# A spiking transformer layer with a gated expert layer: LIF at full width and new places for side work in the first seven beats

## What is computed

```python
def lif_step(v, x_t):                 # leaky integrate and fire
    v = v + (x_t - v) * TAU_INV       # 0.5
    s = spike(v - V_TH)               # 1.0 where v >= 1
    v = v * (1.0 - s)
    return (v, s)

R, K, V = x @ Wr.T, x @ Wk.T, x @ Wv.T          # per step of time:
    vr, r = lif_step(vr, r_in); vk, k = lif_step(vk, k_in); vv, v = lif_step(vv, v_in)
    h = h * DECAY + k * v                       # 0.9
    y = r * h
x1 = layernorm(residual + y @ Wo.T, ln1_g, ln1_b)
h1 = x1 @ W1.T + b1;  s1 = lif_scan(h1)
h2 = s1 @ W2.T + b2;  ffn_out = lif_scan(h2)
attn = layernorm(x1 + ffn_out, ln2_g, ln2_b)
x = _layernorm(x + attn)
x = _layernorm(x + ffn(x))     # softmax gates, best 2 of 8 experts, renormalised
```

## Time and profile before

| | |
|---|---|
| median of 3 runs | 1058.89 us (1058.12 to 1059.48) |
| the profiled execution | 1059.16 us |
| its span | 1057.40 us, 22664 instructions |
| PE busy | 954.4 us (90%) |
| DVE busy | 952.2 us (90%) |
| ACT busy | 551.1 us (52%) |
| POOL busy | 584.8 us (55%) |

### The profile page before, as it was taken

How to read it: one execution, slowest core, us unless ns; L and a number is a source line. 1 busy time by engine, 2 the same in 40 slices (tenths; PEclk the granted TensorE clock), 3 DMA queues, 4 the chain that set the end, 5 groups by cost and what they waited for, 6 DMA issues and landing times.

```text
span 1057.4 us, 22664 instructions
## 1 busy us (share of the span) xinstructions
PE 954.4 (90%) x7552; PEld 929.2 (88%) x7552; DVE 952.2 (90%) x3847; ACT 551.1 (52%) x1270; POOL 584.8 (55%) x726
## 2 busy tenths in 40 slices
PE   4767789999999999999999999999999999898882
PEld 4667779999999999999999999999999999888882
DVE  6898888999999999999999999999999999989861
ACT  4333333555566555555566655555556655455552
POOL 2011112577666666667666666667766666664452
PEclk8778888999999999999999999999999999999996
DMA  4210112454445454445434544544443454456674
GB/s 162 91 51 31 40 31 51 76 105 96 90 86 111 101 110 102 101 91 108 92 88 95 111 101 103 108 98 94 100 93 86 104 103 98 91 100 128 127 136 90
DMA packets 53974, 99.87 MB, mean 94 GB/s; under 512 B 5985, under 2 KB 5985, under 8 KB 53857
## 3 DMA queue, kind: packets, MB, share of 16 engines
q0 software_dynamic: 32256, 58.73, 32.1%
q1 hardware_dynamic: 16992, 31.30, 9.5%
q10 hardware_dynamic: 4608, 8.39, 2.1%
HBM read 31.29 MB, written 8.39 MB: 38 GB/s over the span
## 4 chain that ended last, share of the span: by engine, by line
PE 63%; DVE 26%; DMA 3%; POOL 3%; issue 3%; ACT 2%; POOLq 0%; DVEq 0%; ACTq 0%
PE ps_e L344 28%; PE ps_proj L344 9%; PE ps_proj L414 9%; PE ps_attn L380 6%; PE ps_proj L420 5%; DVE U L713 5%; DVE V L720 4%; DVE stats L794 4%; DVE h L764 2%; PE ps_proj L399 2%; PE ps_attn L388 2%; DVE x1n L821 2%; DVE x1n L806 2%; DMA acc<-term 1%; PE ps_zx L388 1%
## 5 line engine op out<-in xcount | busy, mean ns | idle before, releaser
L344 PE MATMUL ps_e<-we_hi,x_hi 128*128 128x256 f32 (+1 forms) x1024 | 292.8, 286 | 4.0 <-ACT odd_sum L586 4.0
L344 PE MATMUL ps_e<-we_lo,x_hi 128*128 128x256 f32 (+1 forms) x1024 | 287.1, 280 | 0.0
L344 PE MATMUL ps_e<-we_hi,x_lo 128*128 128x256 f32 (+1 forms) x1024 | 287.1, 280 | 0.0
L720 DVE SCALAR_TENSOR_TENSOR V<-U 128x256 f32<-128x256 f32 (+5 forms) x656 | 249.4, 390 | 0.6
L713 DVE SCALAR_TENSOR_TENSOR U<-V,U 128x256 f32<-128x256 f32 (+5 forms) x656 | 234.9, 368 | 1.8
L549 ACT ACTIVATE U<-ps_proj,cst 128x256 f32<-128x256 f32 x320 | 135.6, 481 | 173.1 <-PE ps_proj L420 89.6
L1111 POOL TENSOR_SCALAR veps<-mv 128x2 f32<-128x2 f32 x128 | 56.5, 441 | 295.3 <-DVE mv L800 295.3
L1125 POOL TENSOR_SCALAR s<-U 128x256 fp32r<-128x256 f32 x208 | 192.4, 950 | 10.5 <-DVE V L720 10.5
L344 PEld LDWEIGHTS ps_e<-we_hi,x_hi 128*128 128x128 f32 x1024 | 192.9, 188 | 4.7 <-ACT odd_sum L586 4.6
L344 PEld LDWEIGHTS ps_e<-we_hi,x_lo 128*128 128x128 f32 x1024 | 193.0, 188 | 0.1
L344 PEld LDWEIGHTS ps_e<-we_lo,x_hi 128*128 128x128 f32 x1024 | 192.4, 188 | 0.0
(11 more groups left out here) (85 smaller groups left out, 2185.9 us busy)
## 6 DMA issues: line engine op xcount, KB each, us to landing
acc<-term POOLq DMA_DIRECT2D x96, 256.0 KB, 3.7
odd_sum<-term POOLq DMA_DIRECT2D x96, 256.0 KB, 3.3
xt<-x_T SPq DMA_DIRECT2D x33, 256.0 KB, 2.9
xa<-x_tok SPq DMA_DIRECT2D x32, 256.0 KB, 4.2
xb<-cst SPq DMA_DIRECT2D x32, 256.0 KB, 2.3
xb<-x_tok POOLq DMA_DIRECT2D x32, 256.0 KB, 6.1
out<-res ACTq DMA_DIRECT2D x32, 256.0 KB, 2.1
term<-w SPq DMA_DIRECT2D x8, 256.0 KB, 5.5
```

The source lines that it names most:

```text
L344: mm = pe.matmul(dst, lhs, rhs, start=(i == 0), stop=(i == n - 1))
L720: v.scalar_tensor_tensor(out=V[:, c0:c1], in0=u, scalar=THRESHOLD, in1=u, op0=ALU.is_lt, op1=ALU.mult).then_inc(done, 1)
```

## The change

- In beats 0 to 4 LIF is issued at full width, one instruction where there were two; the property `halves` and the semaphore `lif_half` go.
- In `FILL` beats the spikes of the first layer no longer stand in slot -1 but one tile each in slots 0 to 7 (beats 3 to 6 have them). In `DRAIN` beats they stay in slot -1.
- In `FILL` the sum of the first norm moves from slot 2 to 6, its statistics from 3, 4 to 7, 8, the aggregation from 5 to 9, the normalisation from 9 to 15, `x1_low` from 15 to 23; the second and third norms' work moves by 1 or 2 slots, most gate steps and `add_e0` by 1.

```diff
-FILL = dict(z_sum=-1, y=(-1,) * 5, spikes_h1=-1, fin_sum=-1,
-            gate=(4, 5, 6, 7, 8, 9, 10, 11, 12, 13, 17, 18), add_e0=(14, 15),
-            ln1_sum=2, ln1_stats=(3, 4), ln1_aggr=5, ln1_norm=9, x1_low=15,
-            ln2_stats=(0, 1), ln2_aggr=2, ln2_scale=(6, 7), ln2_add=8,
-            ln3_stats=9, ln3_aggr=10, ln3_shift=16, x3_low=31,
+FILL = dict(z_sum=-1, y=(-1,) * 5, spikes_h1=0, fin_sum=-1,
+            gate=(5, 6, 7, 8, 9, 10, 11, 12, 13, 14, 17, 18), add_e0=(15, 16),
+            ln1_sum=6, ln1_stats=(7, 8), ln1_aggr=9, ln1_norm=15, x1_low=23,
+            ln2_stats=(1, 2), ln2_aggr=3, ln2_scale=(8, 9), ln2_add=10,
+            ln3_stats=11, ln3_aggr=12, ln3_shift=18, x3_low=31,
             fin_add=24, fin_stats=25, fin_aggr=26, fin_shift=31)
...
-            def lif_part(b, c0, c1, first_half):
+            def lif_part(b, c0, c1):
...
-                done = lif_half if first_half else lif
-                before = 2 * STEPS * b.k if first_half else b.value(2 * STEPS, 0)
+                done = lif
+                before = b.value(2 * STEPS, 0)
...
-                    if b.halves:
-                        dve.wait_ge(lif_half, last)
...
-                if b.has(LAG_S) and b.dve_spikes and slot == at["spikes_h1"]:
-                    spikes_h1(b)
+                if b.has(LAG_S) and b.dve_spikes:
+                    if at["spikes_h1"] < 0:
+                        if slot < 0:
+                            spikes_h1(b, range(FK))
+                    elif 0 <= slot - at["spikes_h1"] < FK:
+                        spikes_h1(b, (slot - at["spikes_h1"],))
...
-            def spikes_h1(b):
-
+            def spikes_h1(b, tiles):
 
                 if some(b.w2_fills()):
                     dve.wait_ge(proj_filled, b.w2_fills())
-                for ft in range(FK - b.dve_spikes, FK):
+                for ft in tiles:
...
-                    mid = (c0 + c1) // 2 if b.halves else c0
-                    membrane, reset = lif_part(b, mid, c1, False)
-                    if b.halves:
-                        membrane_half, reset_half = lif_part(b, c0, mid, True)
+                    membrane, reset = lif_part(b, c0, c1)
                     for t in range(STEPS):
-                        if b.halves:
-                            membrane_half(t)
                         membrane(t)
                         side(b, 2 * t)
-                        if b.halves:
-                            reset_half(t)
                         reset(t)
                         side(b, 2 * t + 1)
```

More of the change, by code:

```diff
@@ L119, in edge @@
         return self.k < FIRST_STEADY or self.k > LAST_FULL
-    @property
-    def halves(self):
-        return self.k < LAG_Z
     @property
@@ L249, in build @@
         proj_filled, proj_read = sem("proj_filled"), sem("proj_read")
-        lif, lif_half = sem("lif"), sem("lif_half")
+        lif = sem("lif")
         state_steps = sem("state_steps")
```

## The result

The changed kernel takes 1062.96 us (median of 4 runs, 1062.12 to 1064.47), against 1058.51 for the kernel before on the same chip. The ratio is 1.0057, 95% interval 1.0039 to 1.0076: 4.5 us slower by the medians and 6.0 by the ratio. The forecast was 1061.9, range 1056.5 to 1066.0, with 0.57 on slower. The profiled execution of after took 1062.12, the fastest of the four, for a span of 1060.3. That is 2.9 longer than the span of before (1057.40), so the two traces can locate 2.9 of the 4.5 to 6.

A forecast was written before the change was run, and what follows sets the result against it. DVE and PE waiting for each other bound the fill, PE the middle. Of 8.1 us won by beat 5, 3.1 stay after beat 5; beat 6 loses 6.1: +3.0 on 1058.89, 1061.9, range 1056.5 to 1066.

The forecast's parts named there:

- LIF pace: Beats 0 to 4 on DVE: a 224-column LIF instruction takes 0.30, or 0.43 bare, against a pair at 0.37.
- The 1.05: Fill, slots 0 to 3: one DVE instruction lasts 1.05 longer while POOL's split of x runs.
- 8.1 won by beat 5: Fill: attention of beat 5 starts at 122.6 instead of 130.75 on PE, 8.1 us won.
- W1 behind `x1_low`: Fill beats on PE: W1 takes 7.8 after `x1_low`, with ends 7.5 and 8.9.
- the wait at `ln2_add`: Beats 5 and 6: DVE waits 1.9 and 1.8 at `ln2_add` for POOL's second reciprocal root.
- The gap and the clock: Beat 6: PE idles 4.1 ahead of the x1n transposes, then loses 2.0 at 1.2 GHz.
- The shift: Behind beat 6: PE has no gap and the drain is the same, so the +3.0 stays to the end.
- Rival (a): Fill and beat 6: break-even, low-clock stretches short, W1 of beat 6 +0.5, time 1059.4; chance 0.20.
- Rival (b): Beats 5 and 6: late places are free, norm within 13.5 of attention, 8.1 stay, time 1050.8; chance 0.07.
- Rival (c): Beats 5 and 6: no wait at `ln2_add`, taking off 1.9 and 1.8; 1058.2 or 1056; chance 0.11.
- (d): Low clock in every W1 (8.9 in beats 2 to 4), 2.5 in beat 6; +7.0, time 1065.9; chance 0.16.
- PE's wait ahead of attention: Sign in beats 1 to 4: this wait gone, a wait for the x_lo of `x1_low` in its place.

The follow-up runs named there:

- e1: Kernel before with LIF at full width in beats 0 to 4, all places and spikes as before: 1050.59 us, ratio 0.9926 to before.
- e11: Changed kernel with 32 unused matmuls added in PE's gap of beat 6: 1064.55 us, ratio 1.0061 to before.
- e3: Changed kernel with the old places, spikes included, in beats 5 and 6: 1051.69 us, ratio 0.9946 to before.
- e4: Changed kernel with POOL making the second norm's root ahead of the first's in beats 5 and 6: 1059.18 us, ratio 1.0019 to before.
- e10: e3 with the new places in beat 6 as well, so only beat 5 has the old: 1054.69 us, ratio 0.9969 to before.
- e12: e8 with unused matmuls added in PE's gaps of beats 2 to 5: 1044.30 us, ratio 0.9868 to before.
- e8: Full-width LIF on before, in-between places in beats 0 to 4, old places but second norm's root first in 5 and 6: 1047.10 us, ratio 0.9898.

## Why the prediction was right

The forecast of +3.0 for the end of W1 in beat 6 was +3.65, and +3.0 for the time was +4.5 to +6 (+2.9 in the two spans). The mechanism is shown by the runs. That the first number came so close is in part luck: beats 0 to 4 came out 2.3 later than forecast, beats 5 and 6 1.7 shorter, and the two nearly cancel. Where the time beyond the 2.9 lies, no trace shows. Step by step:

- **LIF pace.** The unseen width of 224 was put at 0.43 bare and 0.30 with side work. After has 0.43 (51.00 to 51.43) and 0.30 (55.02 to 55.32), so the line through 112 and 256 held, and an instruction that needs the result of the one just ahead starts 0.13 later than one that doesn't. The Trainium skill ("VectorE: DVE Perf Modes", Rules for kernel authors) advises fewer operations rather than fewer semaphores; e1 agrees, with 160 fewer and 7.8 us. In another section ("The DRAIN you can't avoid") it says that the semaphore costs nothing extra, from copies issued with a semaphore after each and with one after the last. No run here has an instruction with and without its semaphore, so the 0.13 is the price of the dependence, and the prediction went too far in setting it against that statement.
- **POOL beside DVE.** The 1.05 were 0.95 (the step at 51.86 takes 1.34 where its neighbours take 0.39); by its own rows the prediction should have had 1.08 (1.53 less 0.45). The Trainium skill ("SBUF — State Buffer", SBUF: two separate sides) says that the two engines share a port pair under an exclusive lock, taken for the whole instruction when DVE has two SBUF inputs and POOL reads SBUF. The trace agrees: POOL's split runs from 51.57 to 52.96 in after, and the one DVE step that overlaps its end finishes 0.24 later, at 53.20.
- **Beats 0 to 4.** "8.1 won by beat 5" was 5.8. Beat 1 was right to 0.1; beats 1 to 4 were then 0.5, 0.6, 0.0 and 1.1 longer than the forecast's, 2.2 in all. The count of slots was right: in beat 3 `x1_low` came 15.8 after LIF start (15.9). The term that was too small is W1 behind `x1_low`, put at 7.8: it took 8.5, 8.3, 7.8 and 8.9, and these four differences are the 2.2 to within 0.2. In beats 5 and 6 the sum was too long: `x1_low` came 20.0 after LIF start (20.2), `x3_low` 9.64 behind it (10.5), the wait at `ln2_add` was 1.68 and 1.60 (1.9 and 1.8), the gate's 1.61 (2.3). Beat 5 came out 0.8 shorter than forecast, and beat 6 took 29.7 up to the end of W1 instead of 30.6.
- **The gap and the clock.** The gap was 4.08 (4.1), by two errors that cancel: expert 0 took 1.8 and not 2.4, so W2 ended 0.6 sooner than counted and the transposes came 0.7 sooner too. Behind it the transposes took 0.83 instead of 0.44 and the 36 matmuls 5.61 instead of 4.24, 1.76 together where 2.0 were put down. e11 shows that this comes from the gap: with it filled, the clock is 1.00.
- **The shift.** From beat 7 on nothing changes but the drain, by 0.7.
- **What failed inside it.** The forecast credited the 8.1 to full width and to the late places together. By the times of e1 and e3 the places had no part in it, and in the trace of e1, without them, attention of beat 5 comes 3.4 earlier still. The forecast had seen both sides (waits of 4.8 a beat that go, and the loop that comes; by the earlier trace rows DVE idles only 1.15 of the 2.3 ahead of `ln1_sum`, so they are 3.6) but summed only their total, and so never asked what full width alone would give. The expectation for e1 repeated this, by pricing the instructions (4.5) and not the waits and the low clock that shrink with them (7.8).

Rival (a) fell on W1, 7.8 to 8.9 where it had 7.5, and on the clock of beat 6 (1.76 where it had 1.0); its short `x3_low` (9.9) came true. Rival (b) fell at the point where it was to be decided: the norm of beat 6 started 16.9 after attention (176.08), not within 13.5. Rival (c) fell on the waits of 1.6 to 1.7, though e4 shows its size well: 4.0 without them. Of (d) the low clock in W1 came in part: in after W1 of beat 2 ends 8.3 behind the start of `x1_low` (65.85 to 74.19) and that of beat 3 7.8, but that of beat 4 8.9, as (d) had it (115.74 to 124.66). Of the signs named, PE's wait ahead of attention went in beats 2 to 4 and stayed in beat 1 (8.38).

What stays open: why e10 and e11 differ in the drain, and whether the 1 gained in beat 0 is real, since it can't be told from the scatter of attention of beat 1 (29.3 to 31.0).

## What to carry to other kernels

Moving a step later to let its wait run out is a gain only while the next engine's work behind it is not what the loop waits for: count the loop through both engines, with the moved step's followers, before moving it. Where a change joins a cheaper instruction with new places, price the cheaper one alone first; here it took away 3.4 of the 7.6 of waiting that the places were meant for, and it was worth 7.8 where the whole was worth minus 4.5 to minus 6. A place table should be set per stage: the new one cost 9 to 12 in the two beats with other work in them, and up to 5 in the five before. And where a stage is made faster, look at what starts sooner for it: in e12 the faster W1 moved POOL's work onto the one DVE result that PE waited for.

## What the hardware showed

- Added matmuls in idle time can pay: e12 has 3 us less than e8 (0 to 6), with attention products of 1.99 and 2.00 instead of 3.43 and 3.78 in two beats. In e11, where `x1_low` on DVE came to be waited for, 1.16 of 1.76 arrived at the end of W1 and nothing in the time.
- The same stretch of 84 or 85 matmuls in the drain took 10.5 or 12.1, at a clock of 1.00 or 0.86, behind the same wait of 2.9. This is as large as several of the differences looked for, so the span of one profile should be read by stages.
- One DVE step of 224 columns takes 1.34 instead of 0.39 when POOL's split of 128x512 runs beside it: at 51.86 in after and at 51.28 in e1 (1.35). Which step it is matters: on `y` in e12 it put off attention by 1.14.
